# Slot outputs of two batches in two row tiles, one pair's attention ahead, and a third of the output tiles on ScalarE and GpSimd

## The chip, the core and the metric

One NeuronCore of a Trainium2 chip runs the whole program. The metric is device time in microseconds (us), from launch to the end; lower is better. TensorE is called PE below, VectorE DVE, ScalarE ACT, GpSimd POOL and SyncE SP, as in the profile.

## The reference

Cut to what matters here. Eight batches of 512 rows, each row 512 wide.

```python
x = x + local_attention(ctx, layernorm(x), lengths, positions, W_a, W_c)   # ends in a tanh
h = layernorm(x)
S = slot_init                                        # 64 slots per batch, 512 wide
h1 = gelu(concat(h, mean(S)) @ w1)
alpha = top8_softmax(h1 @ w2)                        # 8 of 64 slots per row
si = (alpha.T @ h) / sum(alpha)                      # slot inputs, per batch
S_new = gru_step(si, S, Wih, Whh)                    # gates r, z, n
q, k, v = S_new @ wq, S_new @ wk, S_new @ wv         # 128, 128, 512 wide
y = layernorm(S_new + softmax(q @ k.T * scale) @ v) * ln_g + ln_b
out = x + (alpha @ (y @ wvp)) @ wo + biases
```

## The kernel before

Everything stays in SBUF. The 4096 rows are 32 tiles of 128 rows, `X[:, t]`; a batch is four tiles, and batches go in four **pairs** (0 to 3), because two batches have 2 x 64 = 128 slots, one partition each. The first 250 us walk over the 32 tiles. The change lies in what follows.

**Gates.** PE computes the gates of the first six batches chunk by chunk (L1252), and then those of the last two, pair 3, in three late gates (L1509, 48 matmuls). `SnT` holds the new slots, transposed; the semaphore `snt` reaches 4 when pairs 0 to 2 have theirs and 5 with pair 3.

**Attention.** For each pair: queries and keys (`query_key`, L1449), values (`values`, L1462), scores, softmax on DVE and ACT, weights turned by PE, then `y_of` (attention times values plus the slots), the layer norm in `norm_y` (statistics on DVE, the power on POOL, the scaling on DVE), `y_turned` (PE transposes), the affine part and the high half on ACT (`turned_y`), the low half on DVE (`y_low`). In the kernel before, queries, keys and scores of pairs 0 to 2 are computed together, and those of pair 3 after them.

**Slot values.** `wvp @ wo` is one matrix `Wp`. Products that need full precision are three passes of a faster format, `mm3` (L303 to L305): high x high, low x high, high x low. `values_of(g)` is 12 such passes for pair g. DVE adds the bias (`SV`), ACT rounds the high half (`SV_hi`), DVE takes the low half (`SV_lo`).

**Outputs.** `out_tiles(g)` makes the eight output tiles of a pair: one tile is `mm3` of 128 slots x 128 rows against `SV`. The 128 slots belong to two batches and a row wants only one, so ACT first writes a copy of alpha with the other batch's half set to zero (`stage`, with `halfmask`, L1120), rounds it (`al_hi`, L1123), and POOL takes the low half (`al_lo`, L516), twice per pair. DVE reads the product from PSUM, scales it by the row's deviation, adds `X` (L895) and puts it into one of eight buffers `ost`; SP sends it (L399). Four PSUM banks go round (`CB`).

The order on each engine is written out by hand; an engine takes its queue strictly in order, and semaphores hold it. SP sends the output tiles in order too.

Of the kernel before, what the change touches and what calls it, by code (L numbers as in the profile page):

```python
# [9 lines left out]
P = 128  # L10
NB, T, D = 8, 512, 512
# [52 lines left out]
def program(nc, d):  # L64
# [87 lines left out]
    region("c2", at_of("xhT"))  # L152
# [15 lines left out]
    region("c3", at_of("xT"))  # L168
    ynT_hi = place("ynT_hi", [P, 2, KC, P], F32R, "c3")
    region("c5", at_of("xT") + 2 * 2 * SLOTS * 4)  # L170
    Wp_hi = place("Wp_hi", [P, KC, D], F32R, "c5")
# [4 lines left out]
    SV = place("SV", [P, NPAIR, D], F32, "c4")  # L176
# [10 lines left out]
    wcs = place("wcs", [P, D], F32, "cm")  # L187
    A2 = place("A2", [P, 2, TPB, 2 * NS], F32, "keep")
# [11 lines left out]
    neghalf, half = small("neghalf", 4), small("halfmask", 2)  # L200
# [52 lines left out]
    region("c2", at_of("xhT"))  # L253
    OST = 8
    ost = place("ost", [P, OST, D], F32, "c2")
    region("c7", at_of("xT") + 2 * SLOTS * 4)
    stage = place("stage", [P, 2, TPB, P], F32, "c7")
# [7 lines left out]
    CB = (banks[2], H0, H1, SI)  # L265
# [3 lines left out]
    LATE, YB, VB = (H0, H1, SI), (H1, SI), (banks[3], banks[6])  # L269
# [47 lines left out]
    def _(sp):  # L317
# [86 lines left out]
    def _(pool):  # L404
        done = [0]

        def link(ins):
# [6 lines left out]
        link(pool.memset(half[:, :], 1.0))  # L414
# [7 lines left out]

        pool.affine_select(out=half[:, 0:1], in_=half[:, 0:1], compare_op=ALU.is_gt, fill=0.0, base=NS,
                           pattern=[[0, 1]], channel_multiplier=-1).then_inc(S("const"), 1)
        pool.affine_select(out=half[:, 1:2], in_=half[:, 1:2], compare_op=ALU.is_ge, fill=0.0, base=-NS,
                           pattern=[[0, 1]], channel_multiplier=1).then_inc(S("const"), 1)
# [77 lines left out]
        pool.wait_ge(S("gn"), 2 * KC)  # L504
        pool.wait_ge(S("snt"), KC)
        for b in range(NB - EB):
            pool.tensor_tensor(late(gd)[:, :, b, :], slotT[:, :, :], late(gn)[:, :, b, :], ALU.subtract).then_inc(S("gd"), 1)
        for g in range(NPAIR):
# [4 lines left out]
        for g in range(NPAIR):  # L513
            for par in range(2):
                pool.wait_ge(S("al_hi"), 2 * g + par + 1)
                pool.tensor_tensor(al_lo[:, par, :, :], stage[:, par, :, :], al_hi[:, par, :, :].bitcast(F32),  # L516
                                   ALU.subtract).then_inc(S("al_lo"), 1)

    @block.vector
    def _(v):  # L520
# [283 lines left out]
        for gate, (dst, name) in enumerate(((gr, "gr_in"), (gz, "gz_in"))):  # L804
# [5 lines left out]
        v.wait_ge(S("gr"), KC + 1)  # L810
        for b in range(NB - EB):
            link(v.scalar_tensor_tensor(late(gn)[:, :, b, :], late(gr)[:, :, b, :], 1.0, ghT[:, 2 * KC:3 * KC, :],
                                        ALU.add, ALU.mult), "zl")
        v.wait_ge(S("gi_late"), 3)
        v.tensor_tensor(gn[:, 0, :], LATE[2], gn[:, 0, :], ALU.add).then_inc(S("gn_in"), 1)
        v.wait_ge(S("in_v"), 48)

        def scores(lo, hi, n):

            v.wait_ge(S("ss"), n)  # L820
            link(v.scalar_tensor_tensor(sc[:, lo:hi, :], s3(banks[2])[:, lo:hi, :], float(DQ) ** -0.5,
# [3 lines left out]
        def weights(lo, hi, n):  # L825
# [4 lines left out]
        def weights_turned(lo, hi, n):  # L830
            v.wait_ge(S("satT"), n)
            v.tensor_copy(atT[:, lo:hi, :], s3(banks[4])[:, lo:hi, :]).then_inc(S("atT"), 1)

        def values(g):

            v.wait_ge(S("v"), g + 1)
            v.tensor_tensor(V[:, g, :], VB[g % 2], bvr[:, :], ALU.add).then_inc(S("vs"), 1)

        def norm_y(g):
            yb = YB[g % 2]  # L840
            v.wait_ge(S("y"), g + 1)
# [767 lines left out]
```

## Time and profile before

| | |
|---|---|
| median of 3 runs | 374.58 us (374.35 to 374.64) |
| profiled execution, its own time | 374.83 us |
| span of that execution | 373.1 us |
| PE busy | 360.0 us, 96% of the span |
| DVE, ACT, POOL busy | 68%, 51%, 47% |

The span runs from the first to the last instruction of the profiled execution; 1.7 us of its own time lie around the span. A line of the page such as `9899` gives the busy tenths of 40 slices of 9.3 us each. A busy PE means that matmuls are in flight, so durations of matmuls overlap: what one costs is read from the start of one to the start of the next.

### The profile page before, as it was taken

The numbers are of one execution on the slowest core, as the hardware profiler recorded it, in microseconds if no ns is written. First come the engines' busy times: TensorE is split into PE (matmuls) and PEld (weight loads), VectorE is DVE, ScalarE is ACT, GpSimd is POOL, SyncE is SP. The second block draws the span as 40 slices with busy tenths as digits, with TensorE's granted clock in tenths as the row PEclk, the third lists the DMA queues.
The fourth block names the chain that finished last, engine by engine and source line by source line (L and its number), as shares of the span: only waits on it lengthen the run. The fifth ranks groups of instructions, "written<-read, shape, count | busy, mean of one in ns | idle before, by whom it ended". The sixth has DMA issues, their size and how long they took to land.

```text
span 373.1 us, 6870 instructions
## 1 busy us (share of the span) xinstructions
PE 360.0 (96%) x2250; PEld 282.7 (76%) x2250; DVE 255.2 (68%) x735; ACT 189.5 (51%) x393; POOL 175.5 (47%) x331
## 2 busy tenths in 40 slices
PE   5899999999999999999999999999999999999996
PEld 2375658999988897988989888876656874667874
DVE  0848986777888787787786886763553335377796
ACT  1260025569668577586595685663422124256241
POOL 2326056887876776677668666440111110014341
PEclk9999999999999999999999999999999999999999
DMA  5899956233132313132322000097000000001488
GB/s 167 269 311 372 355 176 187 62 112 110 60 114 61 112 59 112 59 105 66 93 79 71 16 4 2 0 315 228 3 0 0 2 0 0 3 0 42 185 340 336
DMA packets 41366, 42.78 MB, mean 115 GB/s; under 512 B 3678, under 2 KB 32478, under 8 KB 41331
## 3 DMA queue, kind: packets, MB, share of 16 engines
q1 hardware_dynamic: 39376, 40.42, 32.5%
q10 hardware_dynamic: 1666, 1.27, 1.2%
q0 software_dynamic: 288, 0.66, 0.6%
q8 instruction: 18, 0.29, 0.3%
q14 instruction: 18, 0.14, 0.1%
HBM read 32.18 MB, written 8.39 MB: 109 GB/s over the span
## 4 chain that ended last, share of the span: by engine, by line
PE 70%; DVE 11%; POOL 6%; issue 5%; ACT 4%; DMA 2%; SPq 0%; POOLq 0%; DVEq 0%; ACTq 0%
PE psum L303 11%; PE psum L304 10%; PE psum L305 10%; PE psum L1252 8%; PE psum L1302 5%; PE psum L1462 4%; PE psum L1509 3%; PE psum L1148 3%; PE psum L1330 3%; DMA WvpT<-in_WvpT 2%; PE psum L1190 2%; PE psum L1283 2%; PE psum L1449 2%; POOL X L455 2%; PE psum L1365 1%
## 5 line engine op out<-in xcount | busy, mean ns | idle before, releaser
L303 PE MATMUL psum<-GW_hi,hT_hi 128*128 128x292 f32 (+1 forms) x256 | 79.3, 310 | 1.0 <-POOL GW_lo L437 1.0
L305 PE MATMUL psum<-GW_lo,hT_hi 128*128 128x292 f32 (+1 forms) x256 | 73.9, 289 | 0.0
L304 PE MATMUL psum<-GW_hi,hT_lo 128*128 128x292 f32 (+1 forms) x256 | 73.9, 289 | 0.0
L455 POOL TENSOR_TENSOR X<-X,th 128x512 f32<-128x512 f32 x32 | 38.3, 1196 | 31.5 <-ACT th L985 31.4
L303 PEld LDWEIGHTS psum<-GW_hi,hT_hi 128*128 128x128 f32 x256 | 48.4, 189 | 2.7 <-issue 1.9
L450 POOL TENSOR_TENSOR hT_lo<-xT,hT_hi 128x512 fp32r<-128x512 f32 x32 | 43.4, 1357 | 13.5 <-ACT hT_hi L941 13.5
L304 PEld LDWEIGHTS psum<-GW_hi,hT_lo 128*128 128x128 f32 x256 | 48.4, 189 | 0.2 <-issue 0.2
L305 PEld LDWEIGHTS psum<-GW_lo,hT_hi 128*128 128x128 f32 x256 | 48.1, 188 | 0.0
L303 PE MATMUL psum<-xhT_hi,w_hi 128*128 128x256 f32 x128 | 38.5, 301 | 0.1
L304 PE MATMUL psum<-xhT_hi,w_lo 128*128 128x256 f32 x128 | 36.2, 283 | 0.0
L305 PE MATMUL psum<-xhT_lo,w_hi 128*128 128x256 f32 x128 | 36.1, 282 | 0.0
L1252 PE MATMUL psum<-siT,WihT 128*128 128x384 f32 x96 | 32.3, 489 | 0.0
L303 PEld LDWEIGHTS psum<-xhT_hi,w_hi 128*128 128x128 f32 x128 | 24.3, 190 | 5.9 <-issue 5.9
L697 DVE BATCH_NORM_STATS2 st<-X 128x6 f32<-128x512 f32 x32 | 22.0, 688 | 8.0 <-POOL X L455 7.6
L966 ACT ACTIVATE e<-scm,nmr,rr 128x36 f32<-128x36 f32 x32 | 13.4, 417 | 27.1 <-DVE nmr L693 27.0
L1252 PEld LDWEIGHTS psum<-siT,WihT 128*128 128x128 f32 x96 | 17.7, 190 | 11.6 <-issue 0.8
L980 ACT ACTIVATE xh<-X,nm,r2all 128x512 f32<-128x512 f32 x31 | 24.9, 803 | 1.6 <-POOL nm L464 1.6
L961 ACT CAST xhT_hi<-psum 128x512 fp32r<-128x512 f32 x32 | 18.8, 589 | 13.3 <-PE psum L1330 13.2
L972 ACT CAST aTs<-psum 108x128 fp32r<-108x128 f32 x32 | 8.8, 274 | 32.3 <-PE psum L1355 32.2
L684 DVE TENSOR_TENSOR xhT_lo<-psum,xhT_hi 128x512 fp32r<-128x512 f32 x32 | 21.6, 674 | 5.3 <-ACT xhT_hi L961 4.8
L304 PEld LDWEIGHTS psum<-xhT_hi,w_lo 128*128 128x128 f32 x128 | 24.4, 190 | 0.0
L305 PEld LDWEIGHTS psum<-xhT_lo,w_hi 128*128 128x128 f32 x128 | 24.3, 190 | 0.0
(248 smaller groups left out, 820.2 us busy)
## 6 DMA issues: line engine op xcount, KB each, us to landing
X<-in_x SPq DMA_DIRECT2D x32, 256.0 KB, 3.5
xT<-in_xT SPq DMA_DIRECT2D x32, 256.0 KB, 2.8
out<-ost SPq DMA_DIRECT2D x32, 256.0 KB, 2.9
WhhT<-in_WhhT SPq DMA_DIRECT2D x1, 3072.0 KB, 12.3
WihT<-in_WihT SPq DMA_DIRECT2D x4, 768.0 KB, 8.4
WvpT<-in_WvpT SPq DMA_DIRECT2D x4, 256.0 KB, 8.6
Wo<-in_wo ACTq DMA_DIRECT2D x4, 256.0 KB, 5.7
WaT<-in_WaT SPq DMA_DIRECT2D x1, 1024.0 KB, 11.1
```

The costliest lines, as they stand in the source:

```text
L303: pe.matmul(out, w_hi, m_hi, start=start, stop=False)
L304: pe.matmul(out, w_lo, m_hi, start=False, stop=False)
L305: return pe.matmul(out, w_hi, m_lo, start=False, stop=stop)
L450: pool.tensor_tensor(hT_lo[:, t % 2, :, :], xT[:, t % 4, :, :], hT_hi[:, t % 2, :, :].bitcast(F32), ALU.subtract).then_inc(S("hl"), 1)
L455: pool.tensor_tensor(tile_x(r), tile_x(r), halves(th[:, :]), ALU.add).then_inc(S("x2"), 1)
L684: v.tensor_tensor(xhT_lo[:, :, dst], bank.rearrange("p (c n) -> p c n", c=KC), xhT_hi[:, :, dst].bitcast(F32), ALU.subtract).then_inc(S("x ...
L697: link(v.bn_stats(st2[:, :], tile_x(r)), "stat")
L961: act.copy(xhT_hi[:, :, dst], bank.rearrange("p (c n) -> p c n", c=KC)).then_inc(S("xhh"), 1)
L980: act.activation(halves((th if r == NT - 1 else xh)[:, :]), tile_x(r), ACT.Identity, bias=nm2[:, :], scale=r2all[:, r:r + 1]).then_inc(S(" ...
L1252: last = pe.matmul(RING[gate][:, 0:EN], WihT[:, k, i * P:(i + 1) * P], siT[:, k, 0:EN], start=k == 0, stop=k == KC - 1)
L1302: last = pe.matmul(SI[h * NS:(h + 1) * NS, 0:XW], al, X[:, TPB * b + q, h, :], start=q == 0, stop=q == TPB - 1)
L1462: last = pe.matmul(VB[g % 2], SnT[:, k, g * P:(g + 1) * P], Wv[:, k, :], start=k == 0, stop=k == KC - 1)
```

## The change

1. **Two row tiles.** An output step `outs(m)` now makes two output tiles at once, the same quarter q of both batches of pair g. Each of the three passes is two matmuls, one with the slots of the even batch (partitions 0 to 63), one with those of the odd one (64 to 127), into two PSUM banks. Each contracts over 64 partitions where one tile before contracted over 128. The zeroed copies (`stage`, `halfmask`) are gone: `al_hi` and `al_lo` are made once per pair from `alT`. Two pairs of banks serve (`OB2`); up to step 4 only the first of them, since the other holds `y`.
2. **Pair 0 ahead.** Attention goes as pair 0, then pairs 1 and 2, then pair 3. Output steps and slot values stand between attention steps.
3. **A third of the outputs moved.** Of the output tiles n in the order made, those with n % 3 == 2 are scaled by ACT (`scaled_out`, L1199 of the changed kernel) and `X` is added by POOL (`out`, L547). SP still sends in order of n.
4. **Low halves moved.** `ynT_lo`, `SV_lo` and `Wp_lo` (now four pieces) go from DVE to POOL.

```diff
-    CB = (banks[2], H0, H1, SI)
+    OB2 = ((banks[0], H0), (H1, SI))
+    def out_banks(m):
+        return OB2[m % 2 if m > 4 else 0]
+    def by_pool(n):
+        return n % 3 == 2
...
         for t in range(NT):
-            sp.wait_ge(S("o"), t + 1)
-            sp.dma_start(o_v[:, t, :], ost[:, t % OST, :]).then_inc(S(f"out{t % OST}"), 16)
+            sp.wait_ge(S("op" if by_pool(t) else "o"), of_its_kind(t))
+            sp.dma_start(o_v[:, out_tile(t), :], ost[t % OST][:, :]).then_inc(S(f"out{t % OST}"), 16)
...
+        def low_y(g):
+            pool.wait_ge(S("yhi"), g + 1)
+            pool.tensor_tensor(ynT_lo[:, g % 2, :, :], ynT[:, g % 2, :, :], ynT_hi[:, g % 2, :, :].bitcast(F32),
+                               ALU.subtract).then_inc(S("ylo"), 1)
+        def out(n):
+            t = out_tile(n)
+            pool.wait_ge(S("oa"), of_its_kind(n))
+            pool.tensor_tensor(halves(ost[n % OST][:, :]), halves(ost[n % OST][:, :]), tile_x(t), ALU.add).then_inc(S("op"), 1)
...
+        def scaled_out(n):
+            act.wait_ge(S("oc"), 2 * (n // 2) + 2)
+            wait(act, S(f"out{n % OST}"), 16 * (n // OST))
+            act.activation(ost[n % OST][:, :], out_banks(n // 2)[n % 2], ACT.Identity, scale=dev_of(out_tile(n))).then_inc(S("oa"), 1)
...
+        def outs(m):
+            g, q = m // TPB, m % TPB
+            if q == 0:
+                pe.wait_ge(S("al_lo"), g + 1)
+                pe.wait_ge(S("sv_lo"), g + 1)
+            if m == 5:
+                pe.wait_ge(S("yn"), NPAIR)
+            used = m - 2 if m > 5 else m - 1
+            if m and m != 5:
+                for n in (2 * used, 2 * used + 1):
+                    pe.wait_ge(S("oa" if by_pool(n) else "o"), of_its_kind(n))
+            w_hi, w_lo = al_hi[:, g % 2, q, :], al_lo[:, g % 2, q, :]
+            for n, (w, mv) in enumerate(((w_hi, SV_hi), (w_lo, SV_hi), (w_hi, SV_lo))):
+                for par in range(2):
+                    at_b = slice(par * NS, (par + 1) * NS)
+                    last = pe.matmul(out_banks(m)[par], w[at_b, :], mv[at_b, g, :], start=n == 0, stop=n == 2)
+                    if n == 2:
+                        last.then_inc(S("oc"), 1)
```

What it moves is seen in the engines' queues. PE before, where the weights of pair 3 have been turned (L1480 is the second half of `y_of(3)`, L1489 a `y_turned`, `Wp_hi` the passes of `values_of(1)`, `SV_hi,al_hi` the first output tile):

```order
L1480 MATMUL psum<-ident,SnT 128x128 x4
L1489 MATMUL psum<-ident,yn 128x128 x4
L303 MATMUL psum<-Wp_hi,ynT_hi 128x512
L304 MATMUL psum<-Wp_hi,ynT_lo 128x512
L305 MATMUL psum<-Wp_lo,ynT_hi 128x512
...
L1489 MATMUL psum<-ident,yn 128x128 x4
L303 MATMUL psum<-SV_hi,al_hi 128x512
L304 MATMUL psum<-SV_hi,al_lo 128x512
L305 MATMUL psum<-SV_lo,al_hi 128x512
```

The same place of the change, from output step 3 to the first passes of `values_of(2)` (L1618 the output passes, L1574 and L1576 `y_of(3)`, L1583 `y_turned(2)`):

```order
L1618 MATMUL psum<-SV_hi,al_hi 128x512 x2
L1618 MATMUL psum<-SV_hi,al_lo 128x512 x2
L1618 MATMUL psum<-SV_lo,al_hi 128x512 x2
L1574 MATMUL psum<-V,atT 128x512
L1576 MATMUL psum<-ident,SnT 128x128 x4
L1583 MATMUL psum<-ident,yn 128x128 x4
L1618 MATMUL psum<-SV_hi,al_hi 128x512 x2
L1618 MATMUL psum<-SV_hi,al_lo 128x512 x2
L1618 MATMUL psum<-SV_lo,al_hi 128x512 x2
...
L329 MATMUL psum<-Wp_hi_102,ynT_hi 128x512
```

`y_of(3)`, which stood ahead of every output, now stands behind four output steps and `values_of(1)`; `y_turned(3)` stands behind `values_of(2)`.

POOL's end of the queue before, with all that follows the last statistics:

```order
L510 TENSOR_SCALAR veb<-mrb 128x1
L511 TENSOR_TENSOR mrb<-veb,neghalf 128x1
L516 TENSOR_TENSOR al_lo<-stage,al_hi 128x512 x8
```

POOL's end of the change, from the statistics of pair 3 (L532 `low_y`, L537 `low_alpha`, L542 `low_slot_values`, L547 the moved output tiles; the numbers behind `ost` name buffers):

```order
L528 TENSOR_TENSOR mrb<-veb,neghalf 128x1
L532 TENSOR_TENSOR ynT_lo<-ynT,ynT_hi 128x512
L547 TENSOR_TENSOR ost_109<-ost_109,X 128x512
L537 TENSOR_TENSOR al_lo<-alT,al_hi 128x512
L547 TENSOR_TENSOR ost_196<-ost_196,X 128x512
L542 TENSOR_TENSOR SV_lo<-SV,SV_hi 128x512
L532 TENSOR_TENSOR ynT_lo<-ynT,ynT_hi 128x512
L547 TENSOR_TENSOR ost_199<-ost_199,X 128x512
L537 TENSOR_TENSOR al_lo<-alT,al_hi 128x512
L547 TENSOR_TENSOR ost_110<-ost_110,X 128x512
L542 TENSOR_TENSOR SV_lo<-SV,SV_hi 128x512
L547 TENSOR_TENSOR ost_197<-ost_197,X 128x512
```

The first output tile behind pair 3's slot values that is POOL's (n = 20, `ost_197`) stands behind `SV_lo` of that pair.

## Rows read from the trace of the kernel before

**Rows 1.** The page: busy tenths of PE in 40 slices

```profile
PE   5899999999999999999999999999999999999996
```

**Rows 2.** Timeline of PE from 291 us: start, duration, what [idle before]

```profile
291.16 1.02 PE L1505 MATMUL psum<-rows,ones 128*128 128x512 f32 x2
292.02 10.88 PE L1509 MATMUL psum<-siT,WihT 128*128 128x128 f32 x96
302.73 2.75 PE L1449 MATMUL psum<-SnT,Wq 128*128 128x384 f32 x8
...
307.90 3.60 PE L1462 MATMUL psum<-Wv,SnT 128*128 128x512 f32 x8
311.33 0.83 PE L1455 MATMUL psum<-kT,qT 128*128 128x128 f32 x6
...
320.98 1.02 PE L1478 MATMUL psum<-V,atT 128*128 128x512 f32 x2
...
322.73 0.39 PE L1455 MATMUL psum<-kT,qT 128*128 128x128 f32 x2
...
328.14 0.60 PE L1489 MATMUL psum<-ident,yn 128*128 128x128 f32 x4
328.58 1.02 PE L1478 MATMUL psum<-V,atT 128*128 128x512 f32 x2
...
331.81 0.47 PE L303 MATMUL psum<-Wp_hi,ynT_hi 128*128 128x512 f32 x1 [0.77 <-DVE ynT_lo L851]
...
336.39 0.60 PE L1489 MATMUL psum<-ident,yn 128*128 128x128 f32 x4
```

**Rows 3.** Timeline of PE: first passes of output tiles 4, 8 and 9 [idle before]

```profile
343.40 0.47 PE L303 MATMUL psum<-SV_hi,al_hi 128*128 128x512 f32 x1 [0.19 <-DVE ost L895]
...
351.71 0.39 PE L303 MATMUL psum<-SV_hi,al_hi 128*128 128x512 f32 x1
...
352.39 0.39 PE L303 MATMUL psum<-SV_hi,al_hi 128*128 128x512 f32 x1
```

**Rows 4.** Timeline of DVE: the last 24 output tiles

```profile
353.89 13.35 DVE L895 SCALAR_TENSOR_TENSOR ost<-psum,X 128x512 f32<-128x512 f32 x20
367.56 2.83 DVE L895 SCALAR_TENSOR_TENSOR ost<-psum,X 128x512 f32<-128x512 f32 x4 [0.32 <-PE psum L305]
```

**Rows 5.** A stretch: busy us of PE, PEld, DVE, ACT, POOL (instructions), clock, DMA share, GB/s

```profile
366.00:368.00 2.00, 1.91 (x8) 1.25 (x8) 1.68 (x3) 0.00 (x0) 0.49 (x1) 1.00 1.06 407
```

**Rows 6.** The tile ost: SP's issues, ns min/median/max; landing in us

```profile
L399 SPq DMA_DIRECT2D out<-ost x32: 332/332/2007, 343.3 to 370.4; - x32
...
DMA to landing us min/median/max: 2.0/2.9/4.4
```

**Rows 7.** Timeline of PE: matmuls in two column tiles between whole ones

```profile
273.02 1.96 PE L1302 MATMUL psum<-X,A 128*64 128x258 f32 x16
274.91 2.85 PE L1252 MATMUL psum<-siT,WihT 128*128 128x384 f32 x8
277.60 0.38 PE L1316 MATMUL psum<-ident,sin 128*128 128x128 f32 x2
```

**Rows 8.** Timeline of DVE: statistics and scaling of pair 2

```profile
331.58 0.69 DVE L842 BATCH_NORM_STATS2 stb<-psum 128x6 f32<-128x512 f32 x1
...
333.48 0.81 DVE L846 TENSOR_SCALAR yn<-psum,mrb 128x512 f32<-128x512 f32 x1 [1.00 <-POOL mrb L511]
```

**Rows 9.** Timeline of ACT: affine part and high half of pair 1

```profile
332.11 1.50 ACT L1107 ACTIVATE ynT<-psum,vecs 128x128 f32<-128x128 f32 x4
333.64 0.62 ACT L1110 CAST ynT_hi<-ynT 128x512 fp32r<-128x512 f32 x1
```

**Rows 10.** Groups from 270 us on: busy us, mean ns | idle before, releaser

```profile
L516 POOL TENSOR_TENSOR al_lo<-stage,al_hi 128x512 fp32r<-128x512 f32 x8 | 11.2, 1399 | 16.6 <-ACT al_hi L1123 16.6
...
L858 DVE TENSOR_TENSOR SV<-psum,bpb 128x512 f32<-128x512 f32 x4 | 2.7, 686 | 1.4 <-PE psum L305 1.4
```

**Rows 11.** The page's groups: POOL adds to X, whole span

```profile
L455 POOL TENSOR_TENSOR X<-X,th 128x512 f32<-128x512 f32 x32 | 38.3, 1196 | 31.5 <-ACT th L985 31.4
```

More of the change, by code:

```diff
@@ L175, in program @@
     region("c4", cursor["keep"])
-    SV = place("SV", [P, NPAIR, D], F32, "c4")
+    SV = place("SV", [P, 2, D], F32, "c4")
+    ost = [place(f"ost{i}", [P, D], F32, "c4") for i in range(2)]
     siT = place("siT", [P, KC, SLOTS], F32, "keep")
@@ L503, in _, with scales_y @@
                                gn[:, c % 2, 0:EN].rearrange("p (b s) -> p b s", s=NS), ALU.subtract).then_inc(S("gd"), 1)
[L504 to L508, printed above, removed]
+        def scales_y(g):
             pool.wait_ge(S("agb"), g + 1)
@@ L897, in _ @@
-        out_tiles(0)
-        y_low(3)
+        outs(1)
+        weights(3, 4)
+        stats_y(2)
+        outs(2)
+        norm_y(2)
+        values(3)
+        slot_values(1)
+        weights_turned(3, 4, 3, 3)
+        outs(3)
+        stats_y(3)
+        outs(4)
+        norm_y(3)
+        outs(5)
         slot_values(2)
+        for m in (6, 7, 8):
+            outs(m)
         slot_values(3)
-        for g in range(1, NPAIR):
-            out_tiles(g)
+        for m in range(9, NT // 2):
+            outs(m)
@@ L1512, in _ @@
+        pe.wait_ge(S("te"), NPAIR)
+        pe.wait_ge(S("siv"), NB)
+        late_gate(0)
+        pe.wait_ge(S("bp"), 1)
+        pe.matmul(banks[6], ones[:, :], rows[:, :], start=True, stop=True).then_inc(S("bp_all"), 1)
+        late_gate(1)
         pe.wait_ge(S("snt"), KC)
         pe.wait_ge(S("in_qk"), 32)
-        query_key(0, EN)
+        query_key(0, P)
         pe.wait_ge(S("in_v"), 48)
         values(0)
-        pe.wait_ge(S("qkT"), 2)
-        scores(0, EP)
-        pe.wait_ge(S("bpb"), 1)
@@ L1520, in _ @@
-        for g in range(1, EP):
-            values(g)
-        weights_turned(0, EP, 1)
+        scores(0, 1, 0)
+        query_key(P, EN)
+        weights_turned(0, 1, 1, 1)
+        pe.wait_ge(S("gz_in"), KC + NB - EB)
+        y_of(0)
+        late_gate(2)
+        pe.wait_ge(S("qkT"), 4)
+        y_turned(0)
+        pe.wait_ge(S("bpb"), 1)
+        values(1)
+        values_of(0)
+        scores(1, 3, 2)
+        pe.wait_ge(S("vs"), 2)
+        values(2)
+        weights_turned(1, 3, 2, 0)
@@ L1551, in _ @@
-        out_tiles(0)
-        values_of(2)
+        outs(4)
+        outs(5)
+        pe.wait_ge(S("sv"), 2)
+        values_of(2)
+        pe.wait_ge(S("ynT"), 3 * KC)
+        y_turned(3)
+        for m in (6, 7, 8):
+            outs(m)
         values_of(3)
-        for g in range(1, NPAIR):
-            out_tiles(g)
+        for m in range(9, NT // 2):
+            outs(m)
     ctx.close()
```

374 lines of the change are left out of this document (208 added, 166 removed).

## The prediction

> **What bounds the kernel now.** The page comes first: PE is busy in nine tenths or more of nearly every slice to the end [rows 1]. The timeline of PE then shows why: from 291 us its pieces start as the last ones leave off, though every attention step needs DVE, ACT and POOL in between [rows 2]. The longest stop in these rows is 0.77 us, for a low half. An output tile costs PE 352.39 - 351.71 = 0.68 us [rows 3], and 32 of them 22 us. But PE is not alone in that stretch. DVE moves one tile per 13.35 / 20 = 0.667 us [rows 4]. The stretch from 366 to 368 us shows the DMA engines at a share of 1.06 and 407 GB/s [rows 5]; a tile of 262,144 bytes takes them 0.645 us at that rate. So from 354 us on PE (0.68), DVE (0.667) and DMA (0.645) run side by side, within 6% of each other. Taking work from the first two leaves the third. The last DVE instruction ends at 370.39 us [rows 4], and the span at 373.1, 2.7 us later: 0.33 for SP's issue and 2.0 for a tile that lands with no queue ahead of it [rows 6], and some 0.3 around them.
>
> **The change, part by part.**
>
> *Row tiles.* No row shows matmuls over 64 partitions. The nearest are those in two column tiles: 16 records of 258 columns in 274.91 - 273.02 = 1.89 us, 0.46 ns per column and record, against 2.69 us for 8 records of 384, 0.88 ns [rows 7]. Two of them run at once there, and going over to them and back is inside the 1.89 us. So I take two row tiles as concurrent: three passes of 0.23, 0.69 us for a pair of tiles. The other end is that each half takes its own 0.23, 1.38 us, as much as now. At 0.69 PE saves 16 x 0.69 = 11 us of work. The rule of the Trainium skill ("TensorE: Matmul & The Clock Gate", Part 3) is that tiles in different row groups run at the same time, with a few ns between their starts; by it the price is the 0.69 us of the row. The rule against it ("TensorEngine Tiling (Array Packing)", Key Properties) is that changing the tiling mode drains TensorE. If each of the 13 changes of mode cost PE the 0.08 us by which a first pass after a wait is longer [rows 3], PE would lose 1.0 us, part of it inside its waits, and the sum would come out some 0.5 higher; the trace does not show it at the two changes of the column tiles.
>
> *Where PE's time goes instead.* I lay the queues of the changed kernel beside each other from 291.16 us, with the prices of the rows: late gate 10.71 / 3 = 3.57, bias row 0.86, queries and keys 1.79 for one pair and 3.45 to 3.6 for two, values 3.43, y 1.75, turning y 0.44, a pair's slot values 12 x 0.23 = 2.75 [rows 2, 3]; statistics to scaled y 334.29 - 331.58 = 2.7 [rows 8]; the affine part 1.53 and a high half 0.6 on ACT [rows 9]; SV 0.69, and a low half on POOL 1.31, between the mean of 1.40 of such subtractions [rows 10] and the 1.20 of POOL's additions [rows 11]. A wait of PE costs 0.2 us more, for its release and a first pass of 0.47 instead of 0.39 [rows 3].
>
> - To 308.3: two late gates, bias row, pair 0's queries, keys, values and score, queries and keys of pairs 1 and 2, pair 0's weights, with no wait. Then 0.6 of waiting for atT, y(0) to 310.7, the third gate and turned y(0) to 314.7, V(1) to 318.1. POOL's low half of pair 0 is ready at 318.3, so slot values 0 run from 318.6 to 321.3. Score, V(2), weights, output step 0: 326.1. Waits so far 1.1.
> - 0.5 of waiting, y(1) to 328.35, queries and keys of pair 3 to 330.1. Now the score wants them back from ACT at once: 1.05 of waiting. DVE has the scaling of y(1) in its queue behind that score, so the turning of y(1) waits 1.15 more. y(2), output step 2, V(3), slot values 1 and output step 3 end at 343.1. After 0.5 of waiting y(3) runs 343.6 to 345.4. The same y(3) ended at 336.4 before [rows 2]: of the 9.0 us between, 2.8 are the four output steps and 2.7 the slot values now ahead of it, and 3.5 are waits.
> - y(3) is scaled at 348.3. Output step 5 needs the banks of y, so PE waits 2.0 for it. Slot values 2 wait for POOL's low half (0.4) and end at 352.4; only then is y(3) turned, 4 us after it was ready. ACT takes SV of pair 2 first and ends pair 3's high half at 356.0, POOL the low half at 357.4. PE has had output steps 6 to 8, with 1.2 and 1.4 of waiting around the last. Slot values 3: 357.6 to 360.3. Before, they ended at 351.7 [rows 3]. PE's waits up to here sum to 9.5 us.
>
> *The tail.* Fourteen tiles, 18 to 31, come after slot values 3. Step 9 ends at 361.0, step 10 at 361.7. Tile 20 is ACT's and POOL's. ACT, at the price of a high half, has scaled it at 362.5, but POOL has SV_lo of pair 3 first: slot values 360.3 + 0.2, SV 0.7, high half 0.6, low half 1.3 make 363.1. The addition takes 1.2 [rows 11]: 364.4. SP, in order, holds 21 and 22 behind it. Issue 0.33 and landing 2.0: 366.8. The eleven tiles behind it follow at the DMA's 0.645, 7.1 us: 373.9. DVE, with 10 evictions of 0.667, and PE, with seven steps, are done by 369.4 and 367.4, and cover nothing.
>
> *Hidden edits.* The zeroed copies that ACT drops lay beside a busy PE and give nothing; Wp_lo in four pieces on POOL is done at 303, 15 us before its first use; the two masks stood in POOL's idle start. Were Wp_lo's cover gone, it would cost PE its last piece, 1.3 us.
>
> *The sum.* The queues of the kernel before, laid out with the same prices, end at 372.3, 0.8 us short of the span of 373.1. Most of that lies in the last 15 us; I add 0.6 to 373.9: a span of 374.5, 1.4 more than 373.1. The profiled execution took 374.83 in all, the median 374.58. From the median: **376.0 us**. Prices at their other ends: POOL at 1.5 for each low half and addition adds 1.0; DMA at 0.60 takes off 0.5, at 0.70 adds 0.7; a pair of tiles at 0.9 adds about 0.1, since PE's waits take it up. The likeliest case's own range is 374.8 to 377.3.
>
> **The rivals.**
>
> *The row tiles do not run at once* (0.10). Each step takes 1.38. Nine steps before slot values 3 would add 6.2, but PE's waits hide 4.4; slot values 3 end 1.7 later, and the last seven steps, at 1.38 against 1.29 for two tiles of DMA, set the pace with a last pair to move behind them. The layout then ends 3.1 later: 379.1. For it speaks only that no row has this shape; against it the column tiles.
>
> *The waits before slot values 3 do not come* (0.22), the case on the other side. Its place is pair 3's chain from y(3) to slot values 3, 12.2 us in my layout. If it runs tighter, or POOL and ACT are released earlier than I have them, PE's last three big waits (2.0, 1.2, 1.4) close. Every microsecond that slot values 3 end sooner takes one off the end, since the 14 tiles behind are a fixed 13.6 us. It decides from 0.75 + 1.4 = 2.2 us on, slot values 3 ended by 358.1. With all three closed: 371.4. For it: PE has 11 us less to do, and the kernel before keeps PE fed with the same chains. Against it: the order of the queues. y(3) is turned behind slot values 2 whatever the engines do.
>
> *The outputs leave PSUM in time and the DMA is faster than its rows* (0.08). At 0.5 us per tile the layout ends 1.6 sooner, 374.4, no change: DVE's tiles and the ring of eight buffers hold it then. No row shows over 407 GB/s. This is the limit that the Trainium skill names ("TensorEngine Tiling (Array Packing)", PSUM Bottleneck): tiling speeds up TensorE, not the evacuation of PSUM, which may become the bound. By the rows evacuation has room, with a third moved away, and the transfer has not.
>
> **How the numbers follow.** The likeliest case has 0.60. A measurement here tells about 0.2% from no change: 373.83 to 375.33. Of the likeliest case 0.11 falls inside it, of the second rival 0.04, of the third 0.06. Slower: 0.49 of the first case and 0.10 make 0.59. Faster: 0.18 and 0.02 make 0.20. Same: 0.21. The range from 373.0 to 377.8 leaves out the unconcurrent tiles and the better half of the second rival.
>
> **What would show it.** In the profile after: an output step of six matmuls in 0.69 us, with 11 us less from PE's matmuls of outputs; waits of PE for DVE's `yn`, ACT's `qT` and `kT` and POOL's `ynT_lo`, some 9 us before 358 us; slot values 3 ending near 360; the DMA near 407 GB/s over the last 7 to 10 us; SP waiting for POOL's tiles; and a span of 374.5. I am wrong if PE shows few waits, if the output steps take over 0.9 us each, or if the DMA engines stand idle in the tail while no tile of POOL is late.

## The result, and the profile after

The changed kernel takes 379.01 us (median of 4 runs, 378.69 to 379.95), the kernel before 374.61 in the same series: a ratio of 1.0122 (1.0102 to 1.0141). It is slower, as forecast, but by 4.4 us where 1.4 were forecast, and outside the range. The profiled execution took 379.95 us with a span of 378.1, so 1.85 lie around the span. It is the slowest of the four and has a mean granted clock of 0.984; the three others had spans of 376.8 to 377.2 and 0.992 to 0.993. What follows is read from the slowest run, and the median does not hold all of it.

The page comes first: the busy tenths of PE and the granted clock in 40 slices, the rows that answer to [rows 1].

```profile
PE   5999999999999999999999999999999999888782
PEclk9999999999999999999999999999999999999887
```

PE has lost its nines in the last six slices, where [rows 1] had lost only the last. The clock seems whole until the tail; a slice of 9.5 us hides what comes next. Stretches of 5 us show it: columns are the busy us of PE, PEld, DVE, ACT, POOL (instructions), the granted clock, the DMA share and GB/s.

```profile
340.00:345.00 5.00, 5.00 (x24) 3.30 (x23) 2.57 (x5) 0.62 (x1) 0.60 (x1) 1.00 0.15 56
345.00:350.00 5.00, 3.41 (x25) 2.10 (x23) 2.77 (x5) 3.22 (x7) 2.82 (x5) 0.93 0.27 105
350.00:355.00 5.00, 5.00 (x20) 3.89 (x20) 1.40 (x2) 0.69 (x1) 3.45 (x3) 0.72 0.54 209
355.00:360.00 5.00, 3.05 (x21) 1.95 (x18) 2.86 (x5) 4.33 (x9) 3.45 (x3) 0.96 0.27 105
360.00:365.00 5.00, 5.00 (x21) 3.75 (x21) 0.89 (x2) 0.40 (x1) 2.64 (x3) 0.70 0.54 210
365.00:370.00 5.00, 3.43 (x26) 2.05 (x24) 4.51 (x7) 2.28 (x4) 3.65 (x4) 1.00 0.57 217
370.00:375.00 5.00, 1.28 (x12) 0.74 (x8) 2.30 (x4) 0.69 (x1) 2.35 (x2) 0.82 1.05 405
```

Twice a stretch with a third of PE's time idle or more (3.41 and 3.05 busy of 5) is followed by one in which PE is busy all the time at a clock of 0.72 and 0.70. A busy PE is here a slow PE. The timeline of PE shows both places, pass by pass (L1618 is an output step, L329 to L331 are passes of slot values 2 and then 3).

```profile
343.31 0.40 PE L1618 MATMUL psum<-SV_hi,al_lo 64*128 64x512 f32 x2
343.55 0.39 PE L1618 MATMUL psum<-SV_lo,al_hi 64*128 64x512 f32 x2
343.92 1.13 PE L1574 MATMUL psum<-V,atT 128*128 128x512 f32 x2
...
348.86 0.50 PE L1618 MATMUL psum<-SV_hi,al_hi 64*128 64x512 f32 x2 [1.59 <-DVE yn L920]
...
349.48 0.63 PE L1618 MATMUL psum<-SV_lo,al_hi 64*128 64x512 f32 x2
...
351.06 0.63 PE L331 MATMUL psum<-Wp_lo,ynT_hi 128*128 128x512 f32 x1
351.49 0.63 PE L329 MATMUL psum<-Wp_hi,ynT_hi 128*128 128x512 f32 x1
...
352.77 0.39 PE L329 MATMUL psum<-Wp_hi,ynT_hi 128*128 128x512 f32 x1
353.00 0.39 PE L330 MATMUL psum<-Wp_hi,ynT_lo 128*128 128x512 f32 x1
...
357.27 0.50 PE L1618 MATMUL psum<-SV_hi,al_hi 64*128 64x512 f32 x2 [0.93 <-DVE ost L938]
...
359.25 0.47 PE L329 MATMUL psum<-Wp_hi,ynT_hi 128*128 128x512 f32 x1 [1.02 <-POOL ynT_lo L532]
359.56 0.59 PE L330 MATMUL psum<-Wp_hi,ynT_lo 128*128 128x512 f32 x1
...
362.94 0.43 PE L329 MATMUL psum<-Wp_hi,ynT_hi 128*128 128x512 f32 x1
...
363.76 0.50 PE L1618 MATMUL psum<-SV_hi,al_hi 64*128 64x512 f32 x2
```

Inside an output step the passes start 0.24 us apart (343.31, 343.55): the row tiles run at once, as forecast. From 351.06 to 351.49 the start of one pass to the next takes 0.43 us, and its duration reads 0.63, where 352.77 to 353.00 takes 0.23 with 0.39: half the clock, 1.2 for 2.4 GHz. The first time it is low from just behind the stop of 1.59 us until 352.7, the second from 359.6, behind stops of 0.93 and 1.02, until 362.9. Slot values 3 stand on the path to the end, and end at 363.7 (the layout: 360.3; before: 351.7 [rows 3]).

The tail on DVE, which answers to [rows 4], then POOL's additions after slot values 3, and SP's longest wait for them:

```profile
367.36 2.77 DVE L938 SCALAR_TENSOR_TENSOR ost<-psum,X 128x512 f32<-128x512 f32 x4 [0.49 <-PE psum L1618]
370.63 0.75 DVE L938 SCALAR_TENSOR_TENSOR ost<-psum,X 128x512 f32<-128x512 f32 x1 [0.49 <-PE psum L1618]
372.09 1.41 DVE L938 SCALAR_TENSOR_TENSOR ost<-psum,X 128x512 f32<-128x512 f32 x2 [0.71 <-DMA out<-ost]
```

```profile
365.29 1.27 POOL L542 TENSOR_TENSOR SV_lo<-SV,SV_hi 128x512 fp32r<-128x512 f32 x1 [2.65 <-ACT SV_hi L1187]
366.52 1.20 POOL L547 TENSOR_TENSOR ost<-ost,X 128x512 f32<-128x512 f32 x1
```

```profile
SPq L425 <- POOL ost L547: 20.2, 10, 6.1
```

DVE no longer bounds: it stops for PE and for buffers. POOL adds to tile 20 from 366.52 us, behind its low half, where the layout had 363.1; SP waits for POOL's ten tiles in order (20.2 us in all, 6.1 the longest), and from 370 us the DMA engines run at 405 GB/s. This is the tail of the forecast, 3.4 us later; the transfers are dense for the last 6 us alone, not for 7 to 10.

### The profile page after: what moved, and what is told of

Its sections match the earlier page's. It is cut to its first block and busy times, and to the rows that moved or that the text cites. A ratio compares the mean times of both kernels' runs of the same rounds, so it can differ in the third digit from the quotient of the medians.

```text
span 378.1 us, 6915 instructions
## 1 busy us (share of the span) xinstructions
PE 355.4 (94%) x2266; PEld 276.9 (73%) x2266; DVE 244.5 (65%) x721; ACT 188.1 (50%) x396; POOL 196.8 (52%) x346
## 3 DMA queue, kind: packets, MB, share of 16 engines
q10 hardware_dynamic: 1666, 1.27, 1.1%
## 5 line engine op out<-in xcount | busy, mean ns | idle before, releaser
L329 PE MATMUL psum<-GW_hi,hT_hi 128*128 128x292 f32 (+1 forms) x256 | 79.0, 309 | 1.1 <-POOL GW_lo L457 1.0
L331 PE MATMUL psum<-GW_lo,hT_hi 128*128 128x292 f32 (+1 forms) x256 | 73.9, 289 | 0.0
L329 PEld LDWEIGHTS psum<-GW_hi,hT_hi 128*128 128x128 f32 x256 | 48.4, 189 | 2.9 <-issue 2.0
L331 PEld LDWEIGHTS psum<-GW_lo,hT_hi 128*128 128x128 f32 x256 | 48.1, 188 | 0.0
L329 PE MATMUL psum<-xhT_hi,w_hi 128*128 128x256 f32 x128 | 38.4, 300 | 0.1
L331 PE MATMUL psum<-xhT_lo,w_hi 128*128 128x256 f32 x128 | 36.0, 281 | 0.0
L329 PEld LDWEIGHTS psum<-xhT_hi,w_hi 128*128 128x128 f32 x128 | 24.2, 189 | 5.9 <-issue 5.9
L522 POOL TENSOR_TENSOR gd<-slotT,gn 128x384 f32<-128x384 f32 x4 | 4.0, 997 | 41.9 <-ACT gn L1029 41.9
L1040 ACT CAST xhT_hi<-psum 128x512 fp32r<-128x512 f32 x32 | 18.9, 590 | 12.9 <-PE psum L1427 12.7
```

The source lines that it names most:

```text
L329: pe.matmul(out, w_hi, m_hi, start=start, stop=False)
L331: return pe.matmul(out, w_hi, m_lo, start=False, stop=stop)
L1040: act.copy(xhT_hi[:, :, dst], bank.rearrange("p (c n) -> p c n", c=KC)).then_inc(S("xhh"), 1)
```

## The experiments

Each was timed in five rounds beside the kernel before; "clock" is the mean granted clock of a run, which each run lists.

**1. The stops filled.** Idle matmuls into an unused PSUM bank: 7 ahead of output step 5, 4 ahead of step 8, 5 ahead of slot values 3.

```diff
+        def filler(n):
+            for _ in range(n):
+                pe.matmul(SA, SV_hi[:, 0, 0:P], SV_hi[:, 0, :], start=True, stop=True)
```

> The changed kernel with idle matmuls put on PE where it waits late: 7 passes of 0.23 us before output step 5, 4 before step 8 and 5 before slot values 3, written to a bank nobody reads. Theory A (half clock): PE's granted clock fell to half twice, at 349 and at 359.5 us, each time behind a stretch in which PE had stood still for 1 to 2 us, and 10 and 9 passes then took 0.43 instead of 0.23 us, 1.9 us each time. With the waits filled the clock stays at 1.00, slot values 3 end near 360.3 instead of 363.8, and the time is about 376.0 to 377.0. Rival B (the order of the queues and the transfer alone cost the 4.4 us, the low clock fell into waits anyway): the time stays at 379, perhaps later by what the idle matmuls delay.

Measured: 377.65 us (377.08 to 378.85), ratio 1.0082 (1.0059 to 1.0105), 1.4 less than the changed kernel and 0.65 above the upper end of what was expected. PE does more, and the kernel is faster. The profiled execution has a span of 375.3 and a clock of 1.00 up to 370 us; PE is released at nearly the same moment (step 5 at 348.73, in the changed kernel at 348.86), yet the next stretch is not slow:

```profile
350.00:355.00 5.00, 5.00 (x29) 3.74 (x29) 2.07 (x4) 1.90 (x5) 3.96 (x4) 1.00 0.54 210
```

Slot values 3 run from 358.04 to 360.8 us, against 360.3 in the layout. So the layout was 0.5 short in its chain, and in the profiled run of the changed kernel the rest of the 3.4 us was the clock. These two profiles are the fastest run of one kernel and the slowest of the other: they lie 2.9 us apart, the medians 1.4, about what one fall of the clock costs.

**2 and 3. One half of the filling each.** The 7 alone, and the 4 and 5 alone, by the numbers given to `filler`.

> The changed kernel with the 7 idle matmuls in its first long stop alone (ahead of output step 5, where PE waits 1.6 us for the scaled y of pair 3). Theory A (each of the two falls of the granted clock follows the stop just ahead of it, each costs what it adds on the path): the fall near 349 us goes, the one near 359.6 stays, and the time is half way between the changed kernel and the one with all stops filled: 378.2 to 378.6. Rival B (only the stops after step 7 matter, for slot values 3 alone stand on the path of the tail, while what slot values 2 lose is taken up by PE's later waits): 378.8 to 379.2, no gain. Rival C (one long stop starts it, and the second fall only follows from the first): near the fully filled one, 377.5 to 377.8, with a clock of 1.00 in 355 to 365 us.

> The changed kernel with 4 idle matmuls ahead of output step 8 and 5 ahead of slot values 3, none ahead of step 5. Theory A: the fall near 359.6 us goes, the one near 349 stays: 378.2 to 378.6. Rival B: all of the gain is here, 377.5 to 377.8. Rival C: no gain, the clock is low in 350 to 355 us and again after 358 us: 378.8 to 379.2.

Measured: 378.95 (377.05 to 379.57), ratio 1.0096 (1.0075 to 1.0116), and 378.29 (377.60 to 379.80), ratio 1.0101 (1.0083 to 1.0119). The first lies where rival B put it (378.8 to 379.2) and no lower than the changed kernel, the second where theory A did, and the intervals of both overlap the changed kernel's: the times do not decide. Two of the six runs of the first took 377.05 and 377.26, with a mean clock of 0.997. The traces tell more. With the first stop filled, then with the last two filled:

```profile
350.00:355.00 5.00, 4.89 (x28) 3.66 (x30) 1.44 (x2) 1.52 (x4) 4.37 (x4) 1.00 0.41 157
...
360.00:365.00 5.00, 5.00 (x21) 3.43 (x20) 1.26 (x2) 0.62 (x1) 2.35 (x3) 0.70 0.54 210
```

```profile
350.00:355.00 5.00, 5.00 (x22) 3.85 (x22) 1.44 (x2) 0.73 (x2) 3.32 (x3) 0.76 0.54 210
```

In these two traces the fall behind the filled stop is gone and the other one is there, as theory A has it; rival C falls, since the second fall comes without the first. One trace each is thin ground, because a stop left open does not always bring a fall. Over all traces of the changed kernel and its variants: behind the open stop ahead of step 5 (1.59 to 2.26 us) the clock fell in three of five, behind the filled one in none of three; behind the two open stops around step 8 it fell in three of four, behind the filled ones in neither of two. From PE's turning of pair 2's y to its first pass of slot values 3 the changed kernel takes 359.25 - 345.77 = 13.5 us, the first of these 358.88 - 346.66 = 12.2: a fall is worth 1.3 there, and slot values 2 are on the path to slot values 3 in these traces, against rival B.

**4. The halves apart.** The two loops of an output step exchanged: three passes of the even batch, then three of the odd one.

```diff
-            for n, (w, mv) in enumerate(((w_hi, SV_hi), (w_lo, SV_hi), (w_hi, SV_lo))):
-                for par in range(2):
+            for par in range(2):
+                for n, (w, mv) in enumerate(((w_hi, SV_hi), (w_lo, SV_hi), (w_hi, SV_lo))):
```

> The changed kernel with the loops of an output step exchanged: three passes of the even batch, then three of the odd one, so that neighbours share a row tile. If two row tiles run at once only when they alternate, a step goes from 0.69 to about 1.38 us. By the layout alone that is 3.1 us more. Theory A: PE then waits 4 us less before slot values 3 and its clock does not fall, which gives back up to 3.6, so the time is 378 to 380. Rival B (clock without effect): 382. If the steps take 0.69 in this order too, the exchange changes nothing: 379.

Measured: 379.34 (376.85 to 380.97), ratio 1.0118 (1.0084 to 1.0151), the changed kernel's. The step was not stretched. Its timeline:

```profile
354.01 0.40 PE L1618 MATMUL psum<-SV_hi,al_lo 64*128 64x512 f32 x2
354.24 0.40 PE L1618 MATMUL psum<-SV_lo,al_hi 64*128 64x512 f32 x2
354.48 0.40 PE L1618 MATMUL psum<-SV_hi,al_hi 64*128 64x512 f32 x2
```

A step still takes some 0.7 us, in twos. The test could not make the tiles run one after the other, so it says nothing on what that would cost. Its profile shows something else: nothing was filled or moved, the stop ahead of step 5 is there, and the clock stays whole behind it.

```profile
349.09 0.51 PE L1618 MATMUL psum<-SV_hi,al_hi 64*128 64x512 f32 x2 [1.61 <-DVE yn L920]
...
350.60 0.40 PE L330 MATMUL psum<-Wp_hi,ynT_lo 128*128 128x512 f32 x1
```

The next passes of slot values 2 start 0.23 us apart. The second fall comes (seven passes from 358.25 to 361.37 us), and with that one fall alone the span is 377.1 and the mean clock 0.993, as in the three runs of the changed kernel that were not profiled.

**5. All tiles on DVE.** `by_pool(n)` returns False, and ACT's and POOL's parts drop out; SP waits for DVE alone.

> The changed kernel with all 32 output tiles on DVE, none on ACT and POOL. By the layout, with the order of the queues as the cause, tile 20 no longer waits behind POOL's low half, and the end comes 0.8 us sooner: 378.2. Rival C (evacuation by DVE alone is the limit that the change had to lift, 14 tiles at 0.667 after slot values 3): 1 us or more later, 380. Theory A adds that the clock still falls twice, at the same two places.

Measured: 377.64 (377.49 to 379.97), ratio 1.0072 (1.0052 to 1.0092): 1.4 faster than the changed kernel, against rival C. The third moved away costs here. The profile, of the slowest run, agrees: from the end of slot values 3 (365.2) to the end of the span (378.1) it takes 12.9 us, where the changed kernel took 14.4, and DVE makes the 14 tiles without a stop. That it is tile 20 behind POOL's low half which holds back those behind it fits the layout, which gives 0.8 of the 1.4; the other 0.6 is not explained. The clock did not fall at the same two places: it fell once, for 6.8 us from the end of a stop of 2.26 ahead of step 5, and did not behind the stops of 0.92 and 1.02 us around step 8.

**6. Pair 3's y turned ahead of slot values 2.** On PE, ACT and POOL.

```diff
-        pe.wait_ge(S("sv"), 2)
-        values_of(2)
         pe.wait_ge(S("ynT"), 3 * KC)
         y_turned(3)
+        pe.wait_ge(S("sv"), 2)
+        values_of(2)
```

> The changed kernel with y of pair 3 turned ahead of slot values 2 instead of behind them, on PE, ACT and POOL. By the layout slot values 3 start 0.8 us sooner and the end comes 0.8 sooner. Theory A: the stop of 1.0 us before slot values 3 shrinks, and if the second fall of the clock goes with it, 1.9 us more are gained: 376.3 to 378.2. Rival B: 378.2.

Measured: 376.11 (375.93 to 378.35, 12 runs), ratio 1.0042 (1.0027 to 1.0057): 2.9 less than the changed kernel, more than any other single edit to it. In the profiled execution the stop ahead of step 5 is as long as before, but the clock stays at 1.00 to 370 us:

```profile
348.96 0.49 PE L1618 MATMUL psum<-SV_hi,al_hi 64*128 64x512 f32 x2 [1.59 <-DVE yn L920]
349.85 0.66 PE L1583 MATMUL psum<-ident,yn 128*128 128x128 f32 x4
...
356.17 0.50 PE L1618 MATMUL psum<-SV_hi,al_hi 64*128 64x512 f32 x2 [1.33 <-POOL SV_lo L542]
357.06 0.50 PE L329 MATMUL psum<-Wp_hi,ynT_hi 128*128 128x512 f32 x1
```

Slot values 3 start at 357.06 instead of 359.25. From the turning of pair 2's y to there it takes 357.06 - 345.88 = 11.2 us, where the traces without a first fall (experiments 2 and 4) took 12.2 and 12.3: the order itself is worth 1.0, near the layout's 0.8, and the rest of the 2.9 is falls of the clock that do not come. Eleven of the twelve runs lie between 375.93 and 376.49. The length of a stop does not settle alone whether the clock falls, and since experiment 4 has the same stop and no fall in the order of the change, this profile does not show that the new order is what spared the first one.

**7. The three together.** Experiments 5 and 6, with 6 idle matmuls ahead of step 5 and 5 ahead of step 8.

> The changed kernel with pair 3's y turned ahead of slot values 2, all output tiles on DVE, and idle matmuls in two stops (6 ahead of step 5, 5 ahead of step 8). If the three causes add (the turning 2.9 us, the moved third 1.4 us, and what is left of the clock's falls 0 to 0.5 us): 374.4 to 375.2, no different from the kernel before. If they overlap (the same microseconds after slot values 3 counted twice): 375.3 to 376.1. Under 374 would say that the rest of the change is worth something.

Measured: 376.07 (375.99 to 378.07), ratio 1.0034 (1.0021 to 1.0047), no better than the turning alone and within the second branch. By the time the gains overlap, and the changed order of attention stays 0.34% slower than the kernel before, in the profile with a clock of 1.00 up to 370 us. The spans qualify this: four of the seven runs have 373.1 to 373.7, against 372.5 to 373.4 of the kernel before, and 2.3 to 3.0 us around the span instead of 1.8. In the profiled run the last tiles trickle (one takes 4.0 us to land, in experiment 5 the longest 2.1), and the span is 376.3. Why is open, so it is not settled whether the gains add.

**8. The row tiles alone in the kernel before.** Its attention order, its engines for every step; alpha rounded once a pair, the step of six matmuls, tiles sent in the order made.

```diff
-                mm3(pe, CB[i % 4], al_hi[:, par, q, :], al_lo[:, par, q, :], SV_hi[:, g, :], SV_lo[:, g, :],
-                    True, True).then_inc(S("oc"), 1)
+                for n, (w, mv) in enumerate(((w_hi, SV_hi), (w_lo, SV_hi), (w_hi, SV_lo))):
+                    for par in range(2):
+                        at_b = slice(par * NS, (par + 1) * NS)
+                        last = pe.matmul(CB[2 * (m % 2) + par], w[at_b, :], mv[at_b, g, :], start=n == 0, stop=n == 2)
```

> The kernel before, with its own order of attention and all output tiles and low halves on its own engines; the row tiles alone are put in (alpha rounded once a pair with no zeroed copies, three passes of two matmuls each, four banks in two pairs, tiles sent in the order made). PE does 11 us less in the output stage. Theory: the tail is bound by DVE (32 tiles at 0.67 us) and by the DMA (0.645 us), but slot values 2 and 3 stand between output tiles on PE and come earlier, so that only DVE's own sum is left: from 340.5 us 32 x 0.667 + 4 x 0.7 + 1.3 = 25.4 to 26, its last tile at 367 to 368 instead of 370.4, the span 370 to 371 and the time 372 to 373 (ratio 0.993 to 0.996). Rival 1, nothing, since DVE was the bound already: 374.3 to 374.8. Rival 2, the clock falls in PE's new waits behind DVE (0.6 us in each step) and the time is that of before or more, with a granted clock under 0.98 from 350 us on: 374.5 to 376.

Measured: 375.56 (374.15 to 378.56, 12 runs), ratio 1.0019 (1.0001 to 1.0036). My theory of a gain falls: no run was under 374.15. The median lies in the range of rival 2. The profiled run, the slowest, shows stops of 2.01 us (at 344.18) and 1.90 us (at 358.47) for DVE's evictions, and the clock at 0.50 from 345 to 350 us.

**9. The same with its stops filled,** 7 idle matmuls ahead of output steps 2 and 6. DVE now also waits for both matmul chains of a step before it reads either tile, where experiment 8 had it count tiles; so it is in experiments 10 and 12.

> The row tiles alone in the kernel before, as in the run before this one, and 7 idle matmuls in each of PE's two long stops (ahead of output steps 2 and 6, where it waited 2.0 and 1.9 us for DVE's evictions). Theory: the falls of the clock behind these stops go, slot values 2 and 3 end at 351.8 us, as in the kernel before, and DVE's last 24 tiles run from 354 to 370.3 as before: 374.2 to 374.7, a granted clock of 1.00 to 365 us and a spread between runs under 0.6 us (4.4 us without the idle matmuls). Rival: the row tiles themselves cost something (a drain between modes, a contention), and it stays at 375 or more with the clock at 1.00.

Measured: 374.55 (374.14 to 376.68, 11 runs), ratio 1.0006 (0.9993 to 1.0019), that of before. The spread is 2.5 us, not under 0.6 as expected. DVE's timeline is the reason for the median:

```profile
351.69 0.69 DVE L861 TENSOR_TENSOR SV<-psum,bpb 128x512 f32<-128x512 f32 x1 [0.65 <-PE psum L309]
353.07 0.69 DVE L863 TENSOR_TENSOR SV_lo<-SV,SV_hi 128x512 fp32r<-128x512 f32 x1 [0.69 <-ACT SV_hi L1118]
353.68 15.89 DVE L899 SCALAR_TENSOR_TENSOR ost<-psum,X 128x512 f32<-128x512 f32 x24
```

24 tiles from 353.68 us, as in [rows 4] from 353.89. With that order PE's faster steps only make it wait; what starts the 24 tiles is slot values 3 behind slot values 2, and DVE idles for them.

**10. The row tiles with slot values in the places of the stops.** No idle matmuls.

```diff
-        out_tiles(0)
-        values_of(2)
-        values_of(3)
-        for g in range(1, NPAIR):
-            out_tiles(g)
+        outs(0, 1)
+        values_of(2)
+        outs(2, 3)
+        values_of(3)
+        outs(*range(4, NT // 2))
```

On DVE, `SV` and the low halves of pairs 2 and 3 go between output tiles.

> The row tiles alone in the kernel before, but with slot values 2 and 3 in the places of PE's stops: output steps 0 and 1, slot values 2, steps 2 and 3, slot values 3, steps 4 to 15; DVE takes SV, the low halves and the low half of pair 3's y between output tiles. No idle matmuls. Theory (DVE is the bound of this end of the program, and row tiles are worth what PE's new room lets DVE start earlier): DVE works without a stop from 341.4 us, 32 x 0.667 + 0.75 + 4 x 0.7 = 24.9 us, to 366.3 and with 0.5 to 1 of stops to 367; the time is 371 to 372.3, clock 1.00 to 360 us. Rival: the clock falls in the many stops of 0.3 to 0.6 us behind DVE, or slot values 3 are late: 373.5 to 375.

Measured: 372.94 (372.33 to 373.45), ratio 0.9955 (0.9942 to 0.9969): faster than both kernels, though 0.6 above the forecast's upper end. The profiled run still has a clock of 0.66 from 355 to 360 us, behind a stop of 1.90; by then DVE has a queue, and its last 16 tiles follow with one stop of 0.30 us. This fall, beside a busy DVE, cost little. One control is missing: the new places of slot values without row tiles were not run. By the rows of the kernel before, PE's work from its first output tile on is 32 x 0.68 + 2 x 2.75 = 27.3 us from 340.2 us, to 367.5, and one tile of DVE behind it ends at 368.1, where the last one ended at 370.39. By this estimate the new places alone could bring up to 2.2 us, so that the 1.5 needs the row tiles is not shown.

**11. One stop put into the kernel before.** PE waits for ACT's affine part of pair 3's y ahead of its first output tile.

```diff
+        pe.wait_ge(S("ynT"), NPAIR * KC)
         out_tiles(0)
```

> The kernel before with one stop of PE put in: ahead of its first output tile (340.2 us) PE waits for ACT's affine part of pair 3's y, some 2 us. Nothing else changes. Theory A (a stop of 1.6 to 2 us near the end brings the clock down shortly after PE starts again, with no row tiles in the program): granted clock near 0.5 for some 3 to 5 us between 343 and 349 us, slot values 3 later by the stop and by 2 to 3 us more: 378 to 379.5. Rival B (one stop between two full stretches leaves the clock alone; it needs the part-time work of the changed kernel): the stop alone, 376 to 377, clock 1.00 up to 370 us.

Measured: 378.77 (378.64 to 378.89, 4 runs), ratio 1.0114 (1.0099 to 1.0130). Its timeline of PE:

```profile
343.09 0.80 PE L303 MATMUL psum<-SV_hi,al_hi 128*128 128x512 f32 x1 [2.96 <-ACT ynT L1107]
343.69 0.63 PE L304 MATMUL psum<-SV_hi,al_lo 128*128 128x512 f32 x1
...
345.39 0.63 PE L305 MATMUL psum<-SV_lo,al_hi 128*128 128x512 f32 x1
345.82 0.46 PE L303 MATMUL psum<-SV_hi,al_hi 128*128 128x512 f32 x1
346.12 0.40 PE L304 MATMUL psum<-SV_hi,al_lo 128*128 128x512 f32 x1
```

With no row tile in the program, a single stop of 2.96 us is followed by six passes in 345.82 - 343.09 = 2.73 us. At full clock they take 0.31 + 5 x 0.23 = 1.46. The stop, 1 us longer than I had thought, and the 1.27 lost make 4.2; the kernel is 4.3 slower, and its four runs lie within 0.3 us. Theory A holds, with a shorter slow stretch than I gave it.

**12. Experiment 10 and the moved third.** ACT scales and POOL adds for n % 3 == 2.

```diff
+            sp.wait_ge(S("op" if by_pool(t) else "o"), of_its_kind(t))
+            act.activation(ost[:, n % OST, :], CB[n % 4], ACT.Identity, scale=dev_of(out_tile(n))).then_inc(S("oa"), 1)
+            pool.tensor_tensor(halves(ost[:, n % OST, :]), halves(ost[:, n % OST, :]), tile_x(t), ALU.add).then_inc(S("op"), 1)
```

> As the row tiles with the new places of slot values, and in addition the third of the output tiles (n % 3 == 2) scaled by ACT and added to by POOL, as in the changed kernel; low halves other than alpha's stay on DVE. Theory: where DVE is the bound, moving a third of its tiles away is worth something until the DMA is the bound: tiles go out from 342.3 us, 32 x 0.645 = 20.6 us and 1.7 for the first, so a span of 365 to 368 and 367 to 370 us. Rival: a moved tile passes two engines (0.67 + 1.2 us) and SP sends in order, so each third tile holds back two others; with DVE slowed beside POOL the gain is eaten: 371 to 372.5, as without it.

Measured: 372.27 (371.89 to 372.77), ratio 0.9941 (0.9927 to 0.9954), the fastest of all. The time lies in the rival's range (371 to 372.5), 2.3 above the theory's upper end. The third now brings some 0.7 us at most, and the intervals of experiments 10 and 12 overlap, so that it brings anything is not shown. The DMA engines are at 405 GB/s from 355 to 365 us:

```profile
355.00:360.00 5.00, 3.54 (x24) 1.83 (x20) 3.65 (x6) 2.06 (x3) 3.96 (x5) 1.00 1.05 405
360.00:365.00 5.00, 2.89 (x18) 1.62 (x18) 3.39 (x5) 1.37 (x2) 2.82 (x3) 1.00 1.05 404
```

## Why the prediction was wrong

The sign and the shape were right, the size was not. By its own steps:

- *Row tiles concurrent at 0.69 us*: right. The prediction saw no change of mode in the column tiles' rows; here it is visible, 0.2 us each (below).
- *The order of waits*: right in kind. Those ahead of step 5 (1.59 us, for `yn`), step 8 (0.93) and slot values 3 (1.02, for `ynT_lo`) are in the trace, where the layout had 2.0, 1.2 and 1.4 with their release. All idle times before slot values 3 sum to 6.4 us in the timeline, not to some 9 (the waits that the layout lists add up to 9.3, where it says 9.5).
- *Slot values 3 from 357.6 to 360.3*: **this is the step that failed.** The layout priced a wait at its length plus 0.2 us for the release, and every pass behind it at 0.23 us, a price read where PE never stops. It missed two slow stretches. From 349.48 to 352.77 us seven passes start in 3.29 us, two of them beside the change of mode; at full clock 2 x 0.33 + 5 x 0.23 = 1.81. From 359.56 to 362.94 eight take 3.38, at full clock 1.84. That is 1.5 us apiece, and with 0.4 of the chain's own (y(3) ends at 345.8 instead of 345.4) the 3.4 us by which slot values 3 end late (363.7).
- *The tail*: right. From the end of slot values 3 to the end of the span 378.1 - 363.7 = 14.4 us; the forecast had 374.5 - 360.3 = 14.2.
- *Around the span*: 1.85 us against 1.48, another 0.4. For the profiled execution 3.4 + 0.2 + 0.4 = 4.0, its 379.95 against 376.0.
- *The median*, 3.0 above the forecast, cannot hold both falls: each lasted 3.4 us at half the clock, and 6.8 us of that in a span of 377 alone make a mean of 0.991, where the three other runs have 0.992 and 0.993. One fall, as in the profile of experiment 4, and what the layout was short even with its stops filled (377.08 - 376.0 = 1.1 in the profiled run of experiment 1) make 2.6 of the 3.0.

The sum was also wrong in what I thought of as safe. The case "tiles at 0.9 us would be taken up by PE's waits" treats those waits as room. Experiments 1, 3 and 11 show that they are not free: what PE does in them sets the price of what follows.

The rule in the Trainium skill ("TensorE: Matmul & The Clock Gate", Part 1) is that TensorE's default state is the throttled one and activity releases it. The traces agree in that passes take 0.43 us behind some of the stops and 0.23 wherever the stop was filled; behind other open stops of the same length they take 0.23 as well (experiments 4 and 6). The prediction drew on that page for the row tiles alone, since no row of before had a clock under 1.00; that no row shows a cost, where the change adds what brings it, was no reason for nothing.

Of the rivals none came. *The waits do not come* was wrong as its own "against" said: the waits came, because the order of the queues puts them there. Experiment 6, which turns y(3) ahead of slot values 2, gives back 2.9 us, some 1.0 by the order and the rest by falls that do not come. What makes the change slow is thus more than one thing: the place of that turning with the stops around it, and the moved third (1.4, experiment 5); the parts were not shown to add. With the order of before the row tiles alone cost 0.8 us, or nothing with their stops filled (experiments 8 and 9), and together with new places for slot values they gain 1.5.

Left open: why in experiments 4 and 6 the same stop of 1.6 us leaves the clock whole in the profiled run, and why runs of one kernel differ by up to 4.4 us (374.15 to 378.56 in experiment 8; in 6, 375.93 to 378.35); and what lies around the span in experiment 7.

## What to carry to other kernels

A kernel in which TensorE never stops has prices that hold only while it does not: when a change opens stops of 1 to 3 us, read the granted clock in stretches of a few us behind each, and put real work there (the next independent product), or, failing that, idle matmuls. Look at more than one run: the same stop brings the clock down in one and not in the next. Speeding up an engine whose neighbour works at the same pace moved nothing by itself here (experiment 9); it paid once the order was changed with it, so that the neighbour started earlier (experiment 10), though how much of that the order alone brings was not measured. And a chain that every later output waits for, here pair 3's, is laid out first.

## What the runs showed that I had not expected

**A change between whole and row tiles costs PE 0.2 us.** In experiment 10, slot values 2 after step 1:

```profile
341.54 0.39 PE L1558 MATMUL psum<-SV_hi,al_lo 64*128 64x512 f32 x2
341.76 0.40 PE L1558 MATMUL psum<-SV_lo,al_hi 64*128 64x512 f32 x2
342.09 0.50 PE L307 MATMUL psum<-Wp_hi,ynT_hi 128*128 128x512 f32 x1
342.42 0.40 PE L308 MATMUL psum<-Wp_hi,ynT_lo 128*128 128x512 f32 x1
342.66 0.39 PE L309 MATMUL psum<-Wp_lo,ynT_hi 128*128 128x512 f32 x1
```

The last pass of one mode to the first of the other takes 0.33 us, and that one to the next 0.33, against 0.23 each. In the kernel before the same place, the last output pass to slot values 2, both in whole tiles, has starts at 346.02, 346.26 and 346.49. The changed kernel has 13 such changes, by this price 2.6 us of PE in all (an estimate), partly inside its waits; the prediction had put one at 0.08. The Trainium skill ("TensorEngine Tiling (Array Packing)", Key Properties) says that changing the tiling mode drains TensorE. The traces agree that a change costs time.

**Two row tiles advance by themselves.** With the queue in the order of three passes for one half and then three for the other, both halves' passes still start together (experiment 4, where the two of a pair start 0.01 us apart). So between two row tiles PE does not go strictly by its queue, and whoever reads the results waits for both.

**DVE stands still beside POOL with some operands.** In experiment 10, DVE and POOL:

```profile
350.59 1.41 DVE L903 SCALAR_TENSOR_TENSOR ost<-psum,X 128x512 f32<-128x512 f32 x2
351.91 1.63 DVE L868 TENSOR_TENSOR SV_lo<-SV,SV_hi 128x512 fp32r<-128x512 f32 x1
```

```profile
351.72 1.27 POOL L519 TENSOR_TENSOR al_lo<-alT,al_hi 128x512 fp32r<-128x512 f32 x1 [9.74 <-ACT al_hi L1133]
```

This low half takes 1.63 us, the same one of pair 2, with POOL idle, 0.68. It starts inside POOL's subtraction and ends 0.55 us after it, little less than its own length, as if it had stood still until POOL was through. The evictions, which read PSUM and `X`, keep their pace beside POOL: in the changed kernel three from 364.80 us take 2.07 us, beside POOL's subtraction from 365.29. The Trainium skill ("SBUF — State Buffer", Who interferes with whom) has this as its rule: a DVE instruction with both inputs in SBUF contends with a GpSimd instruction that reads SBUF, and one with a single SBUF input, outside DVE's two-port modes, does not. The traces agree with both halves. In the changed kernel two such operations at 319 and 321 us took 1.70 and 1.64 us beside POOL, in the kernel before 0.69 each.
